# Two chained bottleneck blocks on one core: quad 1's second-block 1x1 as plain float32 products, and the first tile of quad 2 ahead of quad 0's

## The reference

```python
def _L0_conv_ref(x, ...):              # first block, batch norm over all images
    out = relu(_bn(_conv(x, w1, b1, 1, 0), g1, be1))      # 1x1, 512 -> 128
    out = relu(_bn(_conv(out, w2, b2, 1, 1), g2, be2))    # 3x3, 128 -> 128
    out = _bn(_conv(out, w3, b3, 1, 0), g3, be3)          # 1x1, 128 -> 512
    out = softplus(residual_scale)[0] * out
    return relu(x + out)
def _L1_conv_ref(x, ...):              # second block, no norm, scalar biases
    out = _conv(x, w1, 'VALID') + bias1b[0]               # 1x1, 512 -> 128
    out = _conv(out + bias2a[0], w2, 'SAME') + bias2b[0]  # 3x3, 128 -> 128
    out = _conv(out + bias3a[0], w3, 'VALID') + bias3b[0] # 1x1, 128 -> 512
    return relu(out * rscale[0] + rbias[0] + x)
```

## Time and profile before

| what | value |
|---|---|
| three runs | 290.62, 291.74, 291.79 us; median 291.74 |
| the profiled execution, its own time | 290.35 us |
| its span, first to last instruction | 288.3 us |
| outside the span | 2.05 us |
| TensorE (PE) matmuls busy | 271.6 us, 94% of the span |
| VectorE (DVE) busy | 250.2 us, 87% |
| ScalarE (ACT) busy | 203.0 us, 70% |
| mean granted TensorE clock | 0.999 |

### The profile page before, as it was taken

The page is one execution under the profiler, slowest core; times in us unless marked ns, Lnnn a source line. Parts: engine busy times, 40 slices in busy tenths (PEclk is TensorE's granted clock), DMA queues, the critical chain, the costliest instruction groups (busy, mean ns, idle before and its releaser), DMA issues.

```text
span 288.3 us, 4023 instructions
## 1 busy us (share of the span) xinstructions
PE 271.6 (94%) x1534; PEld 253.8 (88%) x1534; DVE 250.2 (87%) x384; ACT 203.0 (70%) x264; POOL 15.9 (6%) x23
## 2 busy tenths in 40 slices
PE   6878999899999998999997999999999999999991
PEld 3668998699999976868796999999999999999991
DVE  3599999999999657789699999999999997979593
ACT  5678883589877549819878783895976949573674
POOL 0000001000000009900000000000000000000000
PEclk9999999999999999999999999999999999999999
DMA  7999901300000010000000000004040050504088
GB/s 229 378 426 422 423 27 50 144 0 2 0 0 2 0 38 2 0 0 3 0 0 0 2 0 2 1 40 183 2 195 28 2 223 0 225 29 195 14 341 316
DMA packets 6818, 28.44 MB, mean 99 GB/s; under 512 B 912, under 2 KB 3472, under 8 KB 5904
## 3 DMA queue, kind: packets, MB, share of 16 engines
q1 hardware_dynamic: 6224, 27.78, 24.2%
q10 hardware_dynamic: 576, 0.41, 0.5%
HBM read 15.35 MB, written 12.85 MB: 98 GB/s over the span
## 4 chain that ended last, share of the span: by engine, by line
PE 79%; DVE 9%; ACT 6%; DMA 3%; issue 1%; SPq 1%; ACTq 0%; DVEq 0%
PE ps L1066 33%; PE ps L1052 18%; PE ps L1018 9%; PE ps L1055 9%; PE ps L1133 4%; DMA x<-x_dram 3%; PE ps L1116 2%; ACT x L556 2%; PE ps L1110 1%; DVE xl L650 1%; DVE xl L875 1%; ACT xh L357 1%; DVE x L870 1%; DVE vf L721 1%; PE ps L1027 1%
## 5 line engine op out<-in xcount | busy, mean ns | idle before, releaser
L511 ACT ACTIVATE x<-x,shift 128x784 f32<-128x784 f32 x32 | 29.9, 946 | 15.4 <-DVE x L870 15.2
L870 DVE SCALAR_TENSOR_TENSOR x<-ps,scale,x 128x784 f32<-128x784 f32 x32 | 32.4, 1030 | 1.3 <-PE ps L1055 1.2
L1066 PE MATMUL ps<-vh,wu0h 128*128 128x364 f32 (+1 forms) x96 | 32.0, 334 | 1.2 <-ACT vh L403 1.2
L1066 PE MATMUL ps<-vh,wu0l 128*128 128x364 f32 (+1 forms) x96 | 32.0, 333 | 0.0
L1066 PE MATMUL ps<-vh,wu1l 128*128 128x364 f32 (+1 forms) x96 | 32.0, 333 | 0.0
L1066 PE MATMUL ps<-vh,wu1h 128*128 128x364 f32 (+1 forms) x96 | 31.9, 333 | 0.0
L912 DVE SCALAR_TENSOR_TENSOR x<-ps,scal,x 128x784 f32<-128x784 f32 x31 | 31.5, 1028 | 0.0
L1066 PE MATMUL ps<-vl,wu0h 128*128 128x364 f32 (+1 forms) x96 | 31.3, 334 | 0.0
L875 DVE TENSOR_TENSOR xl<-x,xh 128x784 fp32r<-128x784 f32 x28 | 26.1, 971 | 5.8 <-ACT xh L518 5.8
L650 DVE TENSOR_TENSOR xl<-x,xh 128x1568 fp32r<-128x1568 f32 x13 | 23.2, 1781 | 1.8 <-ACT xh L357 1.8
L518 ACT ACTIVATE xh<-x 128x1568 fp32r<-128x1568 f32 x14 | 21.1, 1507 | 2.4 <-PE ps L1055 2.4
(11 more groups left out here) (206 smaller groups left out, 714.8 us busy)
## 6 DMA issues: line engine op xcount, KB each, us to landing
x<-x_dram SPq DMA_DIRECT2D x15, 784.0 KB, 8.2
out_dram<-x SPq DMA_DIRECT2D x6, 1568.0 KB, 5.2
out_dram<-x SPq DMA_DIRECT2D x7, 392.0 KB, 2.8
raw<-w_dram SPq DMA_DIRECT2D x1, 1088.0 KB, 5.1
raw<-w_dram SPq DMA_DIRECT2D x1, 576.0 KB, 11.3
raw<-w_dram SPq DMA_DIRECT2D x2, 256.0 KB, 3.1
x<-x_dram ACTq DMA_DIRECT2D x2, 196.0 KB, 4.0
x<-x_dram SPq DMA_DIRECT2D x2, 196.0 KB, 4.2
```

Source lines behind the costliest of these rows:

```text
L511: nc.scalar.activation(x_quad(q, c), x_quad(q, c), ACT.Relu, bias=shift3[:, c:c + 1]).then_inc(x1_ready, 1)
L870: nc.vector.scalar_tensor_tensor(x_quad(q, c), ps[:, bank:bank + 2, 0:N], scale3[:, c:c + 1], x_quad(q, c), ALU.mult, ALU.add).then_inc(s_ ...
L1066: return nc.tensor.matmul(by_row(ps[:, bank, 0:N])[:, :, a:RW - b], wu[part][:, TILE[k] + dw, :], by_row(v[:, k, :])[:, :, b:RW - a], star ...
```

## The change

Quad 1's conv_b becomes plain like quad 0's. Its weights come from a new tile `w1f`, 2 KB per partition, into which SyncE loads the 1x1 weights of the second block a second time (256 KB), right behind the load of `raw1`. With that `high_x(1, 0)`, `high_x(1, 1)` and `low_x(1, 0)` to `low_x(1, 3)` go, and the counts of the semaphores `xh_ready` and `xl_ready` begin with quad 2. `high_x(2, k)` no longer waits for a conv_b.

TensorE's order has conv_a(2, 0) ahead of conv_b(0, 0..3), and conv_a(2, 1..3) behind it. ScalarE does relu1(1, 3) ahead of high_a2(3) and relu1(2, 0) ahead of fill_t1(0). VectorE does v_sums(0, 0) between sum1(2, 0) and sum1(2, 1), and sum1(2, 2) ahead of v_low(0, 1).

```diff
+        w1f_at = region(4 * CT * P)
...
+        w1f = place("w1f", [P, CT, P], F32, w1f_at)
...
             sync.dma_start(raw1[:, :, :], w1_in).then_inc(w1_loaded, 16)
+            sync.dma_start(w1f[:, :, :], w1_in[:, 0:CT]).then_inc(w1f_loaded, 16)
...
             def high_x(q, k):
                 act.wait_ge(x1_ready, CT * q + 2 * k + 2)
-                if q > 1:
+                if q > 2:
                     act.wait_ge(b_done, CT * (q - 1) + 2 * k + 2)
...
             relu1(1, 2)
-            high_x(1, 0)
+            relu1(1, 3)
             high_a2(3)
-            relu1(1, 3)
+            relu1(2, 0)
             fill_t1(0)
-            high_x(1, 1)
-            relu1(2, 0)
             high_v(0, 0)
             relu1(2, 1)
             high_v(0, 1)
...
             sum1(1, 3)
-            low_x(1, 0)
-            low_x(1, 1)
             sum1(2, 0)
+            v_sums(0, 0)
             sum1(2, 1)
-            v_sums(0, 0)
-            low_x(1, 2)
-            low_x(1, 3)
             v_sums(0, 1)
             v_low(0, 0)
             low_a2(3)
+            sum1(2, 2)
             v_low(0, 1)
-            sum1(2, 2)
             sum1(2, 3)
...
+                if q == 1:
+                    if c == 0:
+                        pe.wait_ge(w1f_loaded, 16)
+                        pe.wait_ge(t1_ready, 1)
+                    pe.wait_ge(x1_ready, CT + c + 1)
+                    whole(slot_b(q), w1f[:, c, :], (x[:, 2, c, :], x[:, 3, c, :]), c == 0, c == CT - 1).then_inc(b_done, 1)
+                    return
...
-            for q in range(3):
-                for c in range(CT):
-                    if q > 0:
-                        conv_a(q, c)
-                if q > 0:
-                    for c in range(CT):
-                        conv_b(q - 1, c)
+            for c in range(CT):
+                conv_a(1, c)
+            conv_a(2, 0)
+            for c in range(CT):
+                conv_b(0, c)
+            for c in range(1, CT):
+                conv_a(2, c)
+            for c in range(CT):
+                conv_b(1, c)
```

More of the change, by code:

```diff
@@ L155, in sem @@
             return ctx.enter_context(nc.semaphore(name))
-        par_loaded, w0_loaded, w0u_loaded, w03_loaded, w1_loaded, w3t_loaded = (
-            sem(n) for n in ("par_loaded", "w0_loaded", "w0u_loaded", "w03_loaded", "w1_loaded", "w3t_loaded"))
+        par_loaded, w0_loaded, w0u_loaded, w03_loaded, w1_loaded, w1f_loaded, w3t_loaded = (
+            sem(n) for n in ("par_loaded", "w0_loaded", "w0u_loaded", "w03_loaded", "w1_loaded", "w1f_loaded", "w3t_loaded"))
         x0_loaded = [sem(f"x0_loaded{c}") for c in range(CT)]
@@ L873, in low_x @@
             def low_x(q, c):
-                dve.wait_ge(xh_ready, 2 * (q - 1) + c // 2 + 1)
+                dve.wait_ge(xh_ready, 2 * (q - 2) + c // 2 + 1)
                 nc.vector.tensor_tensor(pair(xl[:, c, :]), x_quad(q, c), pair(xh[:, c, :]).bitcast(F32), ALU.subtract).then_inc(xl_ready, 1)
@@ L1179, in conv_b @@
                     return
-                if q == 1 and c == 0:
+                if q == 2 and c == 0:
                     pe.wait_ge(wb_ready, 1)
-                if q == 1 and c == 0:
-                    pe.wait_ge(t1_ready, 1)
+                if q == 1:
[5 more added lines that the diff above has]
+                    return
                 if q > 1 and c == 0:
@@ L1186, in conv_b @@
                 if c % 2 == 0:
-                    pe.wait_ge(xh_ready, 2 * (q - 1) + c // 2 + 1)
-                tile(slot_b(q), wa1, c, xh[:, c, :], xl[:, c, :], c == 0, c == CT - 1, (xl_ready, CT * (q - 1) + c + 1)).then_inc(b_done, 1)
+                    pe.wait_ge(xh_ready, 2 * (q - 2) + c // 2 + 1)
+                tile(slot_b(q), wa1, c, xh[:, c, :], xl[:, c, :], c == 0, c == CT - 1, (xl_ready, CT * (q - 2) + c + 1)).then_inc(b_done, 1)
             def conv_m(q, k):
```

## The result

| | kernel before | changed kernel |
|---|---|---|
| median of all 14 runs | 291.67 us | 289.95 us |
| lowest run | 290.27 us | 289.66 us |
| the 13 runs that are compared | 4 at 290.3 to 290.6, 9 at 291.2 to 292.1 | 289.66 to 290.64 |
| profiled execution, its own time | 290.35 us | 289.84 us |
| its span | 288.3 us | 288.1 us |

One run of each kernel, of 1522.97 and of 1530.81 us, stands apart from all others and is left out of the comparison.

The account below looks back on a forecast made before the run. TensorE was taken as the bound. New waits of 1.93 us plus 1.00 of work, 2.93, against 2.86 of waits removed gave +0.07 us, put on the median 291.74: 291.8 us, range 289.9 to 292.6.

Parts of the forecast that it names:

- The steps of the stage: Order worked out from conv_a(1,3) to conv_a(3,3): two waits replaced by new ones plus added work, +0.07 us; chance 0.83.
- 3.5 us less for VectorE: Four low_x of quad 1 at 0.885 us each leave VectorE's queue, 3.5 us in all.
- 1.00 more for TensorE: Quad 1's plain product takes 5.27 us where four split tiles took 4.27; 1.00 us added, all on the path.
- the wait of 2.25: TensorE's wait at conv_a(3,1) for sum1(3,0), 1.99 us idle plus 0.26 for starting on a release; forecast to go.
- a new one ahead of conv_a(2,3): New TensorE wait of 1.08 us, as v_sums(0,0) stands ahead of sum1(2,1) on VectorE.
- a new one ahead of conv_a(3,2): New TensorE wait of 0.68 us; conv_a(3,2) was forecast to start at 158.00 against 157.92 before.
- the pair of relu1: relu1(2,2) and relu1(2,3) on ScalarE, behind fill_t1(1) and ahead of high_x(2,1); forecast at 1.89 us.
- The step that failed: Added the +0.07 us to the runs' median of 291.74, not the profiled 290.35, treating the 1.39 us between as run spread.
- The faster one, TensorE closing up: Rival: conv_a(2,3) is released when reached and conv_a(3,2) waits for nothing; 289.9 us on the median; over 0.5% faster: 0.09.
- The slower one: Rival: conv_b(1)'s 1.74 us later end reaches sum1(3,1) in full; 293.5 us on the median, 0.6% slower; chance 0.08.
- a granted clock other than 1.00: Listed sign that the forecast is wrong: TensorE's granted clock leaving 1.00 in this stretch; no size given.
- The price by four passes: Alternative price for quad 1's plain product from the skill's four float32 passes: 5.7 us, sum ending 0.4 us later; not used.

Follow-up runs that it names:

- The order alone: Kernel before with only TensorE's changed loops, quad 1 still split, ScalarE and VectorE orders as before; median 291.03 us, ratio 1.0008.
- The old order: Changed kernel with TensorE's loops of before, conv_b(0) ahead of all of conv_a(2); median 293.41 us, ratio 1.0069 to the kernel before.
- the kernel before, unchanged: Kernel before run again with nothing changed; 12 runs, median 290.96 us, ratio 0.9995; its profiled execution took 291.74 us.

## Why the prediction was wrong

- **The steps of the stage were right.** 3.5 us less for VectorE, 1.00 more for TensorE, the wait of 2.25 gone, a new one ahead of conv_a(2,3), a new one ahead of conv_a(3,2) behind fill_t1(1) in ScalarE's queue: each is in the trace within 0.11 us, and undoing either of the two causes gave what the steps say (0.75 and 0.63 us). Net -0.03 us from the end of conv_a(1,3), where +0.08 was forecast; the pair of relu1 took 1.78 and not 1.89.
- **The step that failed is the one that put the sum on the median**: "The median of the runs shown, 291.74, is 1.39 above the profiled one, a spread that lies in the runs and not in the step." The spread did lie in the step. The trace of before is of the lower group; two of the three runs shown were of the upper one, and those had the clock fall behind the very idle time that the change takes away. I priced the removed idle time at its own length, 2.0 us, and used the granted clock of 1.00 in one trace as if it held for all; the fall of the clock behind it, 1.28 us where it happens, was put at nothing. In the comparison 9 of 13 runs of before are at 291.2 or more: mean of the 13 is 291.30, of its lower four 290.46, so 0.84 us of the gain is the fall of the clock. That share was a high one: in the 73 runs it is 29, at which the fall is worth about 0.5 us (0.4 of 1.28), so the size of the measured gain is in part the draw of these 13.
- **The second part, 0.5 us, was not in the sum at all.** The runs of the changed kernel have a median of 289.93 (the 13), the lower group 290.46. 0.37 of that lies outside the span (1.74 against 2.1), which I carried over unchanged; its cause stays open. The rest, about 0.15, is in the span, as large as the difference between two executions of one kernel.
- The two together are 1.37 us; the difference of the means is 291.30 - 289.98 = 1.32.
- **The rivals.** The faster one, TensorE closing up, did not happen: both of its waits ahead of conv_a(2,3) and conv_a(3,2) are in the trace. The slower one, that the late end of conv_b(1) is passed on in full, did not happen either. No rival had the clock in it, although a granted clock other than 1.00 stood among the signs of being wrong. The price by four passes would have asked for 5.7 us; the plain product of quad 1 took 5.27, from 145.44 to 150.71 us.
- **The range** reached down to 289.9 only for the closed-up case. The measured 289.95 is inside it by luck: TensorE did not close up.

## What to carry to other kernels

If a few runs of a kernel differ by more than a trace explains, look at the granted clock of each run before putting a forecast on their median, and take a trace of each group: here the two groups were executions of the same program in which one idle time of TensorE did or did not cost it the clock. Such an idle time is worth more than its length, and an edit that shortens or fills it (ten matmuls that nobody reads, 0.36% here) gains even where the wait stays. And of a change made of two parts run each alone: here the plain product is worth 0.8% by itself, the new order takes half of it back, through one VectorE instruction placed ahead of another that TensorE waits for.

## What the runs showed of the hardware

- Behind 1.99 us of idle TensorE's granted clock went to 0.50 (1.2 GHz) from about 156.6 to 160 us in the trace of one execution; by their times and mean clocks the same happened in 29 of 73 executions, at a price of 1.28 us each. It also fell behind 2.00 us (5 of 10 runs), behind 2.40 us (6 of 10, at 2.0 us each), and behind 2.08 us near 108 us. With the idle of 1.99 us filled it fell in none of 8. In the changed kernel the longest idle time of TensorE in this stage is 0.81 us, and none of its 13 runs has a clock under 0.993.
- The fall may come at once or a microsecond after TensorE has started again: in two traces ("The order alone", "The old order") the first matmul behind the idle time was already slow, in another (the kernel before, unchanged) the seventh was the first.
- Behind TensorE's last matmul the granted clock falls again, and that costs no time: the runs with it early and late (0.993 and 0.998) have medians within 0.1 us.
- Time outside the span differs by program: 2.05 to 2.19 us in every run of some kernels, 1.69 to 1.81 in others, and eight small VectorE instructions spread it over 1.76 to 2.04. The cause is open.
